# Row statistics of the scan phase on ScalarE instead of VectorE, with one hand-over figure for steps and side work in both phases' orders

## The chip, the cores and the metric

One of the eight cores of a Trainium2 chip runs the whole program. The metric is the device time of one execution in microseconds (us); lower is better. The engines are named as the profile names them: PE is TensorE (PEld its weight loads), DVE is VectorE, ACT is ScalarE, POOL is GpSimd, SP is the engine that issues most DMAs.

## What is computed

Two residual blocks on x of 8 batches x 1024 tokens x 512 channels, all in f32. The first is an attention with 16 heads, whose weights are scaled by the conditioning vector. The second is a gated state-space scan, and the change lies in the computation of `xn` in it:

```python
xr, gate = jnp.split(x @ W_in.T, 2, axis=-1)          # 1024 channels each
xc = silu(conv4(xr + t_emb) + b_conv)
mu = xc.mean(-1, keepdims=True)
var = xc.var(-1, keepdims=True)
xn = (xc - mu) / jnp.sqrt(var + 1e-05) * ln_g + ln_b
Bm, Cm, dt = jnp.split(xn @ W_xproj.T, 3, axis=-1)
dt = jnp.tanh(dt @ W_dt.T + b_dt) * 0.01
Ad = 1.0 + dt * -jnp.tanh(A_log)
Bd = Bm * jnp.minimum(norm(xn), 1.0)
# over the 1024 tokens, state h of 16 x 1024 per batch:
h = clip(h * Ad + Bd * xn_t, -10, 10);  y_t = Cm_t . h
out = (y + D * xn) * silu(gate) @ W_out.T
```

## The kernel before

**Two phases.** `Attention` runs first and `Scan` after it. In each, a planner (`attention_plan`, `scan_plan`) fixes beforehand the order of all pieces of work on every engine. Each engine then works through its own list strictly in order, and waits at a piece until the semaphores of its inputs and buffers have come.

**The scan's steps.** The state of all 8 batches lies on the 128 partitions (8 x 16) with 1024 channels along the row. The recurrence is strictly serial: one step per token, 1024 steps. Step t has four parts.
- `x`, PE line 1794: two matmuls spread the token's row over the partitions, into one of two PSUM buffers (`xps`). It runs two steps ahead, and waits for `q` of step t-2, which frees the buffer.
- `q`, DVE line 2064: state = x * bd + state.
- `g`, DVE line 2070: the clip.
- `out`, PE line 1808: every second step four matmuls contract two states into `yps`; every eighth step ACT evicts that bank (line 1974).

**The side work.** Steps go in 8 chunks of 128 tokens. Beside the steps of chunk i runs side work of two kinds. That of chunk i+1 is its convolution, statistics, projection and rows (`convolve`, `rows`), in two half-batches (`hb`) of four batches (`bb`). That of chunk i-1 is its gates and output projection (`finish`). During the steps all side work has two PSUM banks (`SIDE`). In chunk 0 there is no `finish`, in chunk 7 no `convolve` and no `rows`.

**The statistics of one half-batch.** PE transposes the channels-first result (`t1`, line 1761, 8 groups of four). ACT copies each of the 8 banks to SBUF (`te`, line 1927). DVE takes `bn_stats` of each (`st`, line 2082), `bn_aggr` once per batch (`ag`, line 2087), and adds epsilon (`rs`, line 2096). ACT takes the root (`rsq`, line 1932), DVE the reciprocal and the two factors (`rr`, lines 2100 to 2103). Only then can ACT normalise the rows (`nrm`, line 1938), and DVE finish the projections (`pjo`, lines 2114 and 2117) that PE has left in a bank (`pj`, line 1770).

**What sets the order.** `Order` keeps a modelled clock for each engine and places next the piece that could start first. Each piece has a duration (the second argument of `put`). Side pieces have a due step besides, spread evenly over a range of steps. A piece is ready when its inputs are done, plus a hand-over `lag` if an input comes from another engine; a bank is free a `lag` after its eviction:

```python
engine, end = self.done[piece]
at = max(at, end + (0.0 if engine == item["engine"] else self.lag[item["side"]]))
...
self.free[m] = end + self.lag[item["side"]]
```

`lag` is a pair of microseconds: the first for steps, the second for side work. These figures and the durations are used for the order alone; no instruction carries them.

Of the kernel before, what the change touches and what calls it, by code (L numbers as in the profile page):

```python
# [23 lines left out]
DIN = 1024  # L24
# [5 lines left out]
BANK = 512  # L30
# [1114 lines left out]
def scan_plan(plan, B, NCH, TOK):  # L1145
# [3 lines left out]
    order = Order(plan, 4, (0.2, 0.5))  # L1149
# [46 lines left out]
    def convolve(i, banks, halves=range(2)):  # L1196
        out = []
        put = lambda *a, **k: out.append(item(*a, **k))
        for hb in halves:
# [33 lines left out]
            put("DVE", 0.25, ("rs", i, hb), (("ag", i, hb, HB - 1),) + was("nrm", *old, HB - 1) + was(  # L1233
                "pjo", *old, HB - 1), [("dve_rs", 1)])
            put("ACT", 1.6, ("rsq", i, hb), (("rs", i, hb),), [("act_rs", 1)])
            put("DVE", 0.8, ("rr", i, hb), (("rsq", i, hb),), [("dve_rs", 3)])
# [193 lines left out]
class Scan:  # L1430
    def __init__(self, nc, ctx, d, ident, B, S, first):
# [31 lines left out]
        self.mvb = sb("mvb", [P, HB, 2])  # L1463
        self.rsd = sb("rsd", [P, HB])
# [68 lines left out]
    def dve_signals(self, p):  # L1533
# [4 lines left out]
            "g": "dve_g", "q": "dve_q", "tap": "dve_tap", "st": "dve_st", "ag": "dve_bn", "rs": "dve_rs", "rr": "dve_rs",  # L1538
# [316 lines left out]
    def scalar(self, act):  # L1855
# [5 lines left out]
        for p in plan.pieces:  # L1861
# [59 lines left out]
            elif kind == "te":  # L1921
# [87 lines left out]
    def vector(self, dve):  # L2009
# [6 lines left out]
        for p in plan.pieces:  # L2016
# [72 lines left out]
            elif kind == "rs":  # L2089
                i, hb = at  # L2090
                w.wait_ge(sem["dve_bn"], plan.after("dve_bn", ("ag", i, hb, HB - 1)))
# [4 lines left out]
                dve.tensor_scalar(self.rsd[:, :], self.mvb[:, :, 1], EPS_LN, None, ALU.add).then_inc(sem["dve_rs"], 1)  # L2096
            elif kind == "rr":
# [3 lines left out]
                dve.tensor_scalar(self.nm[:, :], self.mvb[:, :, 0], -1.0, None, ALU.mult).then_inc(sem["dve_rs"], 1)  # L2101
# [228 lines left out]
```

## Time and profile before

| | |
|---|---|
| median of 3 runs | 6392.38 us (6392.36 to 6394.39) |
| the profiled execution | 6391.57 us |
| its span, first to last instruction | 6389.8 us |
| busy: PE / DVE / ACT / POOL | 94 / 71 / 36 / 50 % |
| mean granted PE clock, share of full speed | 0.964 |
| attention with its setup | about 0 to 3345 us |
| the 1024 steps | 3473 to 6299 us |
| the last outputs after the steps | to 6390 us |

Shares of busy time over the whole span mix two phases that have different limits. The page's slices show it: DVE is busy for four to six tenths in the first half and for nine in the second, while PE is at nine in both. So each phase is to be read by itself, and the steps by chunks: their side work repeats from chunk to chunk. [...]

### The profile page before, as it was taken

To read this page: it belongs to the slowest core of one execution; us is meant where nothing else is said; L and a number is where in the kernel's file an instruction comes from. 1 tells how busy PE (TensorE), PEld (TensorE's weight loads), DVE (VectorE), ACT (ScalarE), POOL (GpSimd) and SP (SyncE) were. 2 spreads that over 40 slices of the span, in tenths; PEclk is the share of its full clock that TensorE was granted. 3 is DMA by queue.
4 is the path that set the end of the run, shared out by engine and by line. 5 is a ranking of instruction groups with operands and counts; after the bars stand their busy time and mean duration, and the time that the engine had idled before them with its cause. 6 is when DMAs were issued, how large, how long until landed. Compare 5 with 4: busy or idle time off the path is not lost. (4 is left out here: it accounts for less than half of the span.)

```text
span 6389.8 us, 73140 instructions
## 1 busy us (share of the span) xinstructions
PE 5983.1 (94%) x24000; PEld 2727.2 (43%) x24000; DVE 4526.8 (71%) x5830; ACT 2331.5 (36%) x4460; POOL 3208.2 (50%) x2625
## 2 busy tenths in 40 slices
PE   7999999999999999999986779999999999999998
PEld 3444444444444444444433324444443444444343
DVE  4646556556565555655635999999999999999984
ACT  2444444444444444444444313323232423233111
POOL 1776666767667666675645233424243342424313
PEclk7999999999999999999987989999999999999999
DMA  2332323323233232332214243444444443444433
GB/s 87 84 87 77 95 56 99 87 82 93 60 95 83 82 91 58 96 86 70 72 62 131 65 118 90 141 97 122 117 111 132 100 143 94 126 107 122 116 93 114
DMA packets 411564, 613.29 MB, mean 96 GB/s; under 512 B 58768, under 2 KB 189968, under 8 KB 410672
## 3 DMA queue, kind: packets, MB, share of 16 engines
q1 hardware_dynamic: 374320, 558.24, 31.5%
q10 hardware_dynamic: 36864, 50.38, 3.1%
q8 instruction: 190, 3.11, 0.2%
q14 instruction: 190, 1.56, 0.1%
HBM read 305.31 MB, written 201.38 MB: 79 GB/s over the span
## 5 line engine op out<-in xcount | busy, mean ns | idle before, releaser
L1125 POOL TENSOR_TENSOR acc<-acc,prob 128x512 f32<-128x512 f32 x1536 | 1906.9, 1280 | 920.8 <-PE bank L815 532.3
L1055 DVE TENSOR_REDUCE mx<-bank 128x1 f32<-128x512 f32 x2048 | 1299.2, 683 | 583.8 <-PE bank L785 579.9
L2064 DVE SCALAR_TENSOR_TENSOR g<-xps,bd,g 128x1024 f32<-128x1024 f32 x1024 | 1312.7, 1282 | 156.6 <-PE xps L1794 84.0
L948 ACT ACTIVATE prob<-misc 128x512 f32<-128x512 f32 x1452 | 817.9, 598 | 911.0 <-PE misc L802 732.0
L1794 PE MATMUL xps<-sx,spread 128*128 128x512 f32 x2048 | 888.7, 520 | 181.2 <-DVE g L2064 165.2
L785 PE MATMUL bank<-khat,qhat 96*128 96x512 f32 x2048 | 959.6, 526 | 18.8 <-DVE mx L1055 7.0
L2070 DVE TENSOR_SCALAR g<-g,lim 128x1024 f32<-128x1024 f32 x1024 | 881.0, 860 | 32.3
L802 PE MATMUL misc<-qhat,khat 98*128 98x512 f32 x1642 | 722.5, 475 | 49.2 <-ACT prob L948 43.8
L1794 PEld LDWEIGHTS xps<-sx,spread 128*128 128x128 f32 x2048 | 356.8, 195 | 712.7 <-DVE g L2064 390.5
L1808 PE MATMUL yps<-g,cexp 128*32 128x512 f32 x4096 | 604.8, 640 | 0.0
L785 PEld LDWEIGHTS bank<-khat,qhat 96*128 96x128 f32 x2048 | 384.1, 197 | 497.6 <-issue 383.6
L815 PE MATMUL bank<-prob,V 128*32 128x512 f32 x3584 | 519.5, 628 | 4.3 <-ACT prob L948 4.3
L1751 PE MATMUL miscb<-x2T_sb,w_in 128*128 128x512 f32 x952 | 475.1, 608 | 8.8 <-DMA x2T_sb<-scratch_x2T 8.8
L773 PE MATMUL bank<-xhT,wqk 128*128 128x512 f32 x1024 | 481.6, 602 | 1.0 <-ACT xhT L886 1.0
L802 PEld LDWEIGHTS misc<-qhat,khat 98*128 98x128 f32 x1642 | 312.7, 192 | 363.9 <-ACT prob L948 213.6
L1848 PE MATMUL miscb<-w_out,ygT 128*128 128x512 f32 x928 | 457.0, 603 | 1.4 <-DVE x_t L2168 1.4
L1818 PE MATMUL miscb<-w_in,x2T_t 128*128 128x512 f32 x896 | 434.1, 606 | 1.1 <-DMA x2T_t<-scratch_x2T 1.1
L1074 DVE RECIPROCAL rsum<-rsum 128x512 f32<-128x512 f32 x64 | 214.3, 3349 | 272.3 <-ACT rsum L954 272.3
L2186 POOL TENSOR_TENSOR cexp<-cd,mask 128x256 f32<-128x256 f32 x128 | 79.0, 617 | 648.4 <-DVE g L2070 456.7
L2225 POOL TENSOR_TENSOR y_t<-y_t,dx_t 128x512 f32<-128x512 f32 x118 | 150.7, 1279 | 450.9 <-DVE g L2070 297.0
L1046 DVE SCALAR_TENSOR_TENSOR halves<-bank,qk_dc,halves 128x512 fp32r<-128x512 f32 x128 | 95.7, 748 | 359.3 <-ACT halves L912 359.3
L2193 POOL TENSOR_TENSOR xn<-xn,affine 128x512 f32<-128x512 f32 x128 | 167.2, 1311 | 345.9 <-ACT xn L1938 211.6
(220 smaller groups left out, 6943.1 us busy)
## 6 DMA issues: line engine op xcount, KB each, us to landing
sx<-scratch_xhl SPq DMA_DIRECT2D x512, 128.0 KB, 4.9
scratch_dx<-dx SPq DMA_DIRECT2D x64, 512.0 KB, 2.8
scratch_xhl<-xhi SPq DMA_DIRECT2D x64, 512.0 KB, 4.3
scratch_xhl<-xn SPq DMA_DIRECT2D x64, 512.0 KB, 4.7
scratch_y<-ysb SPq DMA_DIRECT2D x512, 64.0 KB
dx_t<-scratch_dx SPq DMA_DIRECT2D x59, 512.0 KB, 6.1
y_t<-scratch_y SPq DMA_DIRECT2D x59, 512.0 KB, 4.0
xt_n<-in_x SPq DMA_DIRECT2D x112, 256.0 KB, 2.9
```

Source lines behind the costliest of these rows:

```text
L773: mm = pe.matmul(bank[m][:, 0:QC], self.wqk[:, n, it, :], self.xhT[:, it, c * QC:(c + 1) * QC], start=it == 0, stop=it == HT - 1)
L785: pe.matmul(bank[m][:, 0:QC], self.qhat[0:96, s, h, qt * P:(qt + 1) * P], self.khat[0:96, s, h, c * QC:(c + 1) * QC], start=True, stop=Tru ...
L802: pe.matmul(bank[m][:, 0:QC], self.khat[0:98, s, h, kt * P:(kt + 1) * P], self.qhat[0:98, s, h, c * QC:(c + 1) * QC], start=True, stop=Tru ...
L815: mm = pe.matmul(bank[6 + a][h * DH:(h + 1) * DH, 0:QC], self.value(b, kt, g)[:, h * DH:(h + 1) * DH], of, start=kt == 0, stop=kt == TT - 1)
L948: act.activation(to, bank[m][:, 0:QC], ACT.Exp, scale=SCALE).then_inc(sem[f"act_m{m}"], 1)
L1055: dve.tensor_reduce(self.mx2[:, h * TT + qt, c:c + 1], bank[m][:, 0:QC], AX.X, ALU.max).then_inc(sem[f"dve_m{m}"], 1)
L1125: pool.tensor_tensor(self.acc[:, a, h, :], self.acc[:, a, h, :], self.prob[:, (n % 2) * GH + h, :], ALU.add).then_inc(sem["pool_acc"], 1)
L1751: mm = pe.matmul(bank[m][:, :], self.w_in[:, it, ct * P:(ct + 1) * P], self.x2T[:, it, :, :].rearrange("p b q -> p (b q)"), start=it == 0, ...
L1794: mm = pe.matmul(self.xps[t % 2][:, half * BANK:(half + 1) * BANK], self.spread[:, 2 * part + half, :], self.sx[:, n % 2, wd, :], start=Tr ...
L1808: mm = pe.matmul(bank[2 + m][32 * j:32 * (j + 1), :], self.cexp[:, h, tc, :], self.g[:, (t + tp) % 4, half * BANK:(half + 1) * BANK], star ...
L2064: dve.scalar_tensor_tensor(self.g[:, t % 4, :], self.xps[t % 2][:, :], self.bd[:, i % 2, tl:tl + 1], self.g[:, (t - 1) % 4, :], ALU.mult, ...
L2070: dve.tensor_scalar(self.g[:, t % 4, :], self.g[:, t % 4, :], self.lim[:, i % 2, 0, tl:tl + 1], self.lim[:, i % 2, 1, tl:tl + 1], ALU.min, ...
```

## The change

1. In chunks 1 to 7 (`i > 0`) `st` and `ag` are gone from DVE. ACT's copy `te` also gives the sum of each half row (`accum_out`, function Identity in place of Copy). DVE makes the negated mean `nm` of the four batches in two small instructions (`mu`). ACT then squares the centred rows, one ACTIVATE of 128x1024 per batch with the mean as bias and a sum as second output (`sv`); the written squares go to `junk`. `rs` makes the variance from these sums. `rr` has one instruction less, since `nm` exists already. Chunk 0's statistics stay as they were.
2. Both planners take 0.2 us for the hand-over of side work, in place of 0.5.
3. The planner is told of a duration of 0.7 for `te`, 1.06 for each `sv`, 0.25 for `mu`, 0.4 for `rr`.

```diff
-    order = Order(plan, 8, (0.2, 0.5))        # attention_plan
+    order = Order(plan, 8, (0.2, 0.2))
...
-    order = Order(plan, 4, (0.2, 0.5))        # scan_plan
+    order = Order(plan, 4, (0.2, 0.2))
...
-                    put("ACT", 0.6, ("te", i, hb, bb, half), (g,) + was("slo", *old, bb), [("act_m{m}", 1)],
-                        group=g, give=True)
-                    put("DVE", 0.7, ("st", i, hb, bb, half), (("te", i, hb, bb, half),) + (
-                        (("ag", i, hb, bb - 2),) if bb > 1 else ()), [("dve_st", 1)])
-                put("DVE", 0.2, ("ag", i, hb, bb), (("st", i, hb, bb, 1),), [("dve_bn", 1)])
+                    put("ACT", 0.6 if i == 0 else 0.7, ("te", i, hb, bb, half), (g,) + was("slo", *old, bb) + (
+                        was("mu", *old) if i > 1 or i and hb else ()), [("act_m{m}", 1)], group=g, give=True)
...
+                put("DVE", 0.25, ("mu", i, hb), (("te", i, hb, HB - 1, 1),) + was("pjo", *old, HB - 1), [("dve_bn", 2)])
+                for bb in range(HB):
+                    put("ACT", 1.06, ("sv", i, hb, bb), (("mu", i, hb),), [("act_sq", 1)])
+                stats = ("sv", i, hb, HB - 1)
...
+                    act.activation(to, bank[m][:, :], ACT.Identity, accum_out=self.sums[:, bb, half:half + 1]).then_inc(
+                        sem[f"act_m{m}"], 1)
+            elif kind == "sv":
+                i, hb, bb = at
+                w.wait_ge(sem["dve_bn"], plan.after("dve_bn", ("mu", i, hb)))
+                w.wait_ge(sem["act_sq"], plan.before("act_sq", p))
+                w.wait_ge(sem["dve_rs"], plan.after("dve_rs", ("rs", i - 1 + hb, 1 - hb)))
+                act.activation(self.junk[:, :], self.xn[:, bb, :], ACT.Square, bias=self.nm[:, bb:bb + 1],
+                               accum_out=self.dev[:, bb:bb + 1]).then_inc(sem["act_sq"], 1)
...
+                    w.wait_ge(sem["act_sq"], plan.after("act_sq", ("sv", i, hb, HB - 1)))
...
+                    dve.tensor_scalar(self.rsd[:, :], self.dev[:, :], 1.0 / DIN, EPS_LN, ALU.mult, ALU.add).then_inc(
+                        sem["dve_rs"], 1)
+            elif kind == "mu":
...
+                dve.tensor_tensor(self.nm[:, :], self.sums[:, :, 0], self.sums[:, :, 1], ALU.add).then_inc(sem["dve_bn"], 1)
+                w.wait_ge(sem["dve_bn"], plan.after("dve_bn", p) - 1)
+                dve.tensor_scalar(self.nm[:, :], self.nm[:, :], -1.0 / DIN, None, ALU.mult).then_inc(sem["dve_bn"], 1)
```

**What moves in the orders.** First DVE's list during chunk 3, steps 36 and 37 of its 128, where the first half-batch of chunk 4 has its statistics. Before:

```order
L2064 SCALAR_TENSOR_TENSOR g<-xps,bd,g 128x1024
L2082 BN_STATS st<-xn 128x6
L2087 BN_AGGR mvb<-st 128x2
L2070 TENSOR_SCALAR g<-g,lim 128x1024
L2064 SCALAR_TENSOR_TENSOR g<-xps,bd,g 128x1024
L2082 BN_STATS st<-xn 128x6 x2
L2087 BN_AGGR mvb<-st 128x2
L2082 BN_STATS st<-xn 128x6
L2070 TENSOR_SCALAR g<-g,lim 128x1024
L2082 BN_STATS st<-xn 128x6
L2087 BN_AGGR mvb<-st 128x2
L2096 TENSOR_SCALAR rsd<-mvb 128x4
```

And with the change, steps 38 to 42 (the two `nm` rows are `mu`, the `rsd<-dev` row is `rs`, the last row begins `rr`):

```order
L2137 TENSOR_TENSOR nm<-sums 128x4
L2139 TENSOR_SCALAR nm<-nm 128x4
L2096 TENSOR_SCALAR g<-g,lim 128x1024
L2090 SCALAR_TENSOR_TENSOR g<-xps,bd,g 128x1024
L2096 TENSOR_SCALAR g<-g,lim 128x1024
L2090 SCALAR_TENSOR_TENSOR g<-xps,bd,g 128x1024
L2096 TENSOR_SCALAR g<-g,lim 128x1024
L2128 TENSOR_SCALAR rsd<-dev 128x4
L2090 SCALAR_TENSOR_TENSOR g<-xps,bd,g 128x1024
L2096 TENSOR_SCALAR g<-g,lim 128x1024
L2090 SCALAR_TENSOR_TENSOR g<-xps,bd,g 128x1024
L2143 RECIPROCAL rsd<-rsd 128x4
```

The statistics' instructions that stood between the step's are gone. Between `mu` and `rs` now stand three clips and two `q`, and `rs` and `rr` come three steps later than before.

ACT's list at the same half-batch, with the change:

```order
L1945 ACTIVATE xn,sums<-miscb 128x512 x4
L1953 ACTIVATE junk,dev<-xn,nm 128x1024 x4
L2000 ACTIVATE ysb<-yps 128x512
L2030 ACTIVATE ygT<-miscb 128x512
L1958 ACT_TABLE_LOAD
L1958 ACTIVATE rsd<-rsd 128x4
L1964 ACTIVATE xn<-xn,nmr_b,rsd 128x1024 x2
```

The four `sv` stand together, ahead of an eviction of `yps` and one of a side bank. Before, the last copies, one eviction, the table load and the root followed one another. In the whole list of ACT 67 table loads stand with the change, and 53 before.

PE's list with the change, from the `x` of steps 38 and 39 to the `x` of step 44 (`wx,xc` is `pj`, `ident,y_t` a transpose of `finish`; both kinds take a side bank):

```order
L1805 MATMUL xps<-sx,spread 128x512 x4
L1781 MATMUL miscb<-wx,xc 128x48 x4
L1819 MATMUL yps<-g,cexp 32x512 x4
L1805 MATMUL xps<-sx,spread 128x512 x2
L1781 MATMUL miscb<-wx,xc 128x48 x4
L1851 MATMUL miscb<-ident,y_t 128x128 x4
L1805 MATMUL xps<-sx,spread 128x512 x2
L1819 MATMUL yps<-g,cexp 32x512 x4
L1805 MATMUL xps<-sx,spread 128x512 x2
L1781 MATMUL miscb<-wx,xc 128x48 x8
L1805 MATMUL xps<-sx,spread 128x512 x2
L1819 MATMUL yps<-g,cexp 32x512 x4
```

Before, the first two projections stood within one step (8 and 8 matmuls around one `out`), and output matmuls of `finish` followed three steps later; now the second projection waits for a bank some three steps after the first, and PE's list holds little but steps' matmuls in between. Attention's lists move too, by the second part of the change alone, without a piece more or less.

## Rows read from the trace of the kernel before

**Rows 1.** The page, busy time, share and instructions of each engine, whole span
```profile
PE 5983.1 (94%) x24000; PEld 2727.2 (43%) x24000; DVE 4526.8 (71%) x5830; ACT 2331.5 (36%) x4460; POOL 3208.2 (50%) x2625
```

**Rows 2.** Busy time by stretch (start:end, length, engines with counts, PE clock, DMA share, GB/s)
```profile
0.00:3345.00 3345.00, 3195.80 (x12745) 1463.89 (x12746) 1867.77 (x2833) 1435.33 (x2641) 2140.00 (x1729) 0.97 0.28 81
800.00:3200.00 2400.00, 2330.27 (x9486) 1071.20 (x9478) 1378.29 (x2083) 1046.05 (x1919) 1604.36 (x1295) 0.99 0.28 80
3473.00:6299.00 2826.00, 2639.77 (x10758) 1182.19 (x10757) 2597.81 (x2901) 827.69 (x1688) 944.63 (x798) 0.97 0.42 110
```

**Rows 3.** The same view, chunks 0, 3 and 7 of the steps
```profile
3473.00:3810.00 337.00, 257.17 (x1085) 105.80 (x1083) 322.96 (x370) 94.42 (x201) 91.62 (x80) 0.91 0.31 78
4535.00:4896.00 361.00, 345.29 (x1411) 157.16 (x1410) 333.56 (x378) 115.60 (x237) 133.84 (x112) 0.98 0.44 117
5982.00:6297.00 315.00, 308.83 (x1208) 131.79 (x1210) 271.42 (x263) 39.44 (x65) 49.46 (x46) 0.99 0.39 93
```

**Rows 4.** The same view, chunk 3 in eight pieces of 16 steps each
```profile
4535.00:4579.00 44.00, 44.00 (x160) 18.66 (x159) 40.48 (x43) 14.08 (x37) 6.36 (x6) 1.00 0.49 114
4579.00:4623.00 44.00, 43.33 (x166) 18.82 (x165) 41.73 (x45) 13.97 (x38) 6.35 (x6) 1.00 0.28 69
4623.00:4677.00 54.00, 51.95 (x250) 27.32 (x248) 48.68 (x64) 19.44 (x37) 18.20 (x15) 1.00 0.44 102
4677.00:4726.00 49.00, 48.20 (x178) 20.57 (x180) 46.52 (x48) 19.97 (x45) 23.12 (x19) 1.00 0.38 105
4726.00:4773.00 47.00, 45.26 (x205) 23.42 (x202) 45.57 (x64) 20.29 (x41) 19.90 (x18) 0.93 0.54 159
4773.00:4818.00 45.00, 42.12 (x177) 19.18 (x176) 36.70 (x39) 8.89 (x12) 21.59 (x19) 0.92 0.34 83
4818.00:4857.00 39.00, 34.32 (x134) 13.59 (x133) 36.95 (x34) 8.68 (x13) 21.74 (x18) 0.96 0.57 171
4857.00:4896.00 39.00, 36.10 (x153) 15.62 (x152) 36.92 (x47) 10.29 (x16) 16.57 (x14) 1.00 0.48 142
```

**Rows 5.** Waits (engine line <- releaser: us in all, times, longest), chunk 3
```profile
PE xps L1794 <- DVE g L2064: 13.1, 16, 1.9
...
DVE g L2064 <- PE xps L1794: 7.3, 8, 2.8
```

**Rows 6.** Groups by line, VectorE, chunk 3 (busy us, mean ns | idle us before)
```profile
L2082 DVE BATCH_NORM_STATS2 st<-xn 128x6 f32<-128x512 f32 x16 | 10.8, 681 | 0.0
...
L2087 DVE BATCH_NORM_AGGREGATE mvb<-st 128x2 f32<-128x12 f32 x8 | 1.7, 207 | 0.2
...
L2096 DVE TENSOR_SCALAR rsd<-mvb 128x4 f32<-128x4 f32 x2 | 0.3, 170 | 0.1
```

**Rows 7.** VectorE in order of time at the last steps (start us, us)
```profile
6265.52 1.29 DVE L2064 SCALAR_TENSOR_TENSOR g<-xps,bd,g 128x1024 f32<-128x1024 f32 x1
6266.84 0.81 DVE L2070 TENSOR_SCALAR g<-g,lim 128x1024 f32<-128x1024 f32 x1
6267.74 1.28 DVE L2064 SCALAR_TENSOR_TENSOR g<-xps,bd,g 128x1024 f32<-128x1024 f32 x1
```

**Rows 8.** Groups by line, ScalarE, chunk 3
```profile
L1927 ACT ACTIVATE xn<-miscb 128x512 f32<-128x512 f32 x16 | 9.3, 596 | 15.3 <-PE miscb L1761 15.3
...
L1953 ACT ACTIVATE junk<-xn 128x1024 bf16<-128x1024 f32 x8 | 8.4, 1047 | 0.0
...
L1953 ACT ACTIVATION_READ_ACCUMULATOR junk<-xn 128x1 f32 x8 | 1.5, 192 | 0.0
L1932 ACT ACT_TABLE_LOAD x1 | 1.3, 1283 | 0.0
```

**Rows 9.** In order of time: a transpose eviction and the weight load behind it
```profile
4400.48 0.60 ACT L1927 ACTIVATE xn<-miscb 128x512 f32<-128x512 f32 x1 [1.39 <-PE miscb L1761]
...
4401.13 0.42 PEld L1761 LDWEIGHTS miscb<-ident,xc 128*128 128x128 f32 x4 [0.24 <-ACT xn L1927]
```

**Rows 10.** Waits of PE for data, attention from 800 to 3200 us
```profile
PE misc L802 <- ACT prob L948: 29.3, 80, 0.9
```

More of the change, by code:

```diff
@@ L1227, in convolve @@
                     put("PE", 0.45, g, (("silu", i, hb, 4 * half + 3),), [("pe_m{m}", 1)], take=banks, group=g)
[L1228 to L1234 removed]
+                    put("ACT", 0.6 if i == 0 else 0.7, ("te", i, hb, bb, half), (g,) + was("slo", *old, bb) + (
+                        was("mu", *old) if i > 1 or i and hb else ()), [("act_m{m}", 1)], group=g, give=True)
+                    if i == 0:
+                        put("DVE", 0.7, ("st", i, hb, bb, half), (("te", i, hb, bb, half),) + (
+                            (("ag", i, hb, bb - 2),) if bb > 1 else ()), [("dve_st", 1)])
+                if i == 0:
+                    put("DVE", 0.2, ("ag", i, hb, bb), (("st", i, hb, bb, 1),), [("dve_bn", 1)])
+            if i == 0:
+                stats = ("ag", i, hb, HB - 1)
+            else:
+                put("DVE", 0.25, ("mu", i, hb), (("te", i, hb, HB - 1, 1),) + was("pjo", *old, HB - 1), [("dve_bn", 2)])
+                for bb in range(HB):
+                    put("ACT", 1.06, ("sv", i, hb, bb), (("mu", i, hb),), [("act_sq", 1)])
+                stats = ("sv", i, hb, HB - 1)
+            put("DVE", 0.25, ("rs", i, hb), (stats,) + was("nrm", *old, HB - 1) + was("pjo", *old, HB - 1), [("dve_rs", 1)])
             put("ACT", 1.6, ("rsq", i, hb), (("rs", i, hb),), [("act_rs", 1)])
[L1236 removed]
+            put("DVE", 0.8 if i == 0 else 0.4, ("rr", i, hb), (("rsq", i, hb),), [("dve_rs", 3 if i == 0 else 2)])
             for bb in range(HB):
@@ L1254, in rows @@
                 if bb < HB:
-                    put("ACT", 1.06, ("nrm", i, hb, bb), (("rr", i, hb), ("st", i, hb, bb, 1)), [("act_nm", 1)])
+                    put("ACT", 1.06, ("nrm", i, hb, bb), (("rr", i, hb),), [("act_nm", 1)])
                     for half in range(2):
@@ L1463, in __init__ @@
         self.mvb = sb("mvb", [P, HB, 2])
+        self.sums = sb("sums", [P, HB, 2])
+        self.dev = sb("dev", [P, HB])
         self.rsd = sb("rsd", [P, HB])
@@ L1926, in scalar @@
                     w.wait_ge(sem[f"st_xlo{bb}"], plan.after(f"st_xlo{bb}", ("slo", i - 1 + hb, 1 - hb, bb)))
-                act.activation(self.xn[:, bb, half * BANK:(half + 1) * BANK], bank[m][:, :], ACT.Copy).then_inc(
-                    sem[f"act_m{m}"], 1)
+                to = self.xn[:, bb, half * BANK:(half + 1) * BANK]
+                if i == 0:
+                    act.activation(to, bank[m][:, :], ACT.Copy).then_inc(sem[f"act_m{m}"], 1)
+                else:
+                    if i > 1 or hb:
+                        w.wait_ge(sem["dve_bn"], plan.after("dve_bn", ("mu", i - 1 + hb, 1 - hb)))
+                    act.activation(to, bank[m][:, :], ACT.Identity, accum_out=self.sums[:, bb, half:half + 1]).then_inc(
[7 more added lines that the diff above has]
+                               accum_out=self.dev[:, bb:bb + 1]).then_inc(sem["act_sq"], 1)
             elif kind == "rsq":
@@ L2090, in vector @@
                 i, hb = at
-                w.wait_ge(sem["dve_bn"], plan.after("dve_bn", ("ag", i, hb, HB - 1)))
+                if i == 0:
+                    w.wait_ge(sem["dve_bn"], plan.after("dve_bn", ("ag", i, hb, HB - 1)))
+                else:
+                    w.wait_ge(sem["act_sq"], plan.after("act_sq", ("sv", i, hb, HB - 1)))
                 if i or hb:
@@ L2095, in vector @@
                     w.wait_ge(sem["dve_pr"], plan.after("dve_pr", ("pjo", i - 1 + hb, 1 - hb, HB - 1)))
-                dve.tensor_scalar(self.rsd[:, :], self.mvb[:, :, 1], EPS_LN, None, ALU.add).then_inc(sem["dve_rs"], 1)
+                if i == 0:
+                    dve.tensor_scalar(self.rsd[:, :], self.mvb[:, :, 1], EPS_LN, None, ALU.add).then_inc(sem["dve_rs"], 1)
+                else:
+                    dve.tensor_scalar(self.rsd[:, :], self.dev[:, :], 1.0 / DIN, EPS_LN, ALU.mult, ALU.add).then_inc(
+                        sem["dve_rs"], 1)
+            elif kind == "mu":
+                i, hb = at
+                for bb in range(HB):
+                    for half in range(2):
+                        self.of_bank(w, "act", ("t1", i, hb, bb, half), ("te", i, hb, bb, half))
+                w.wait_ge(sem["dve_pr"], plan.after("dve_pr", ("pjo", i - 1 + hb, 1 - hb, HB - 1)))
+                w.wait_ge(sem["dve_rs"], plan.after("dve_rs", ("rr", i - 1 + hb, 1 - hb)))
+                dve.tensor_tensor(self.nm[:, :], self.sums[:, :, 0], self.sums[:, :, 1], ALU.add).then_inc(sem["dve_bn"], 1)
+                w.wait_ge(sem["dve_bn"], plan.after("dve_bn", p) - 1)
+                dve.tensor_scalar(self.nm[:, :], self.nm[:, :], -1.0 / DIN, None, ALU.mult).then_inc(sem["dve_bn"], 1)
             elif kind == "rr":
```

5 lines of the change are left out of this document (3 added, 2 removed).

## The prediction

> **What bounds the kernel now.** The page's busy shares come first [rows 1]: PE 94%, DVE 71%, ACT 36%, POOL 50%. ACT, which gets the work, has the most room. The shares mix two phases, so the busy times by stretch come next [rows 2]. In attention PE is busy 2330.3 of 2400 us and DVE 1378 of them: PE bounds, and what DVE does there is hidden. Over the 2826 us of steps PE has 2639.8 and DVE 2597.8, which says that two engines stand near the limit.
>
> The same view by chunk [rows 3] tells the chunks apart. Chunk 0 has no output work: PE 257 of 337 us, DVE 323. It is DVE's. Chunk 3, which stands for chunks 1 to 6 (361.0 to 363.0 us each), has PE at 345.3 and DVE at 333.6 of 361. Chunk 7 has PE at 308.8 of 315 and no statistics. In eight pieces of 16 steps [rows 4] chunk 3 shows which engine ends last where. In the first four PE leaves 0, 0.7, 2.0 and 0.8 us, and DVE 3.5, 2.3, 5.3 and 2.5. In the fifth both are nearly full. In the last three PE leaves 2.9, 4.7 and 2.9. The waits [rows 5] show the coupling: PE waits 13.1 us for `q` to free a buffer, DVE 7.3 us for `x`; the rest of DVE's 27 us without work are short gaps and waits that this view counts elsewhere. The third and the fifth piece hold the two half-batches' statistics (54 and 47 us where 39 are possible).
>
> **What leaves DVE.** Per half-batch 8 `st` of 0.681 and 4 `ag` of 0.207 go: 5.45 + 0.83 = 6.28 us [rows 6]. `mu` brings two instructions of 128x4 and `rr` loses one; `rs` keeps its size. Net one tiny instruction more, at the 0.170 of the nearest row [rows 6]. That is 6.11 us per half-batch, 12.2 per chunk. Chunks 1 to 7 are prepared beside chunks 0 to 6, so 14 half-batches: **85.5 us less work on DVE**. It lies between the steps' own instructions and nothing else covers it there; the question is what PE lets through.
>
> - *Chunk 0.* PE has 80 us free, so the 12.2 come back almost whole. The longer ACT chain may take a little: 11 us.
> - *Chunks 1 to 6, lower end.* If PE's work stays in its pieces, the two pieces with statistics can shrink only by PE's free time, 2.05 + 1.74 = 3.8 us per chunk [rows 4].
> - *Upper end.* 12.2 per chunk, if PE's side work slips into the last three pieces, where PE has 10.5 us free.
> - *Taken: 7 per chunk, 42 in all*, a little below the middle of 3.8 and 12.2. Side work is due by the step and steps come sooner, so the planner asks PE for the same work in less time. The five early pieces already fill PE, and PE's total of 345.3 us forbids a chunk much under 350 unless switching between kinds of matmul gets cheaper.
> - *Chunk 7.* Only the order changes: 0, with 3 us either way.
>
> **What ACT gets.** Each `te` gains a read of the accumulator, 0.192 [rows 8]; each `sv` is a 128x1024 ACTIVATE with its read, 1.047 + 0.192 = 1.24 us, since `junk<-xn` is the same form. Per half-batch 8 x 0.192 + 4 x 1.24 = 6.5 us, 91 us in all, beside 115.6 us of work in 361 us [rows 3]: hidden. What isn't hidden is latency. DVE's list has `rs` behind `mu` with three clips and two `q` between. At the bare step's pace, 2.22 us [rows 7], those take 0.81 + 2 x 2.22 = 5.25 us. ACT needs 4 x 1.24 = 4.96 and two hand-overs. A hand-over shows as 0.05 us: the eviction ends at 4401.08 and the weight load starts at 4401.13 [rows 9]. So 5.06 against 5.25: the planner counts 1.06 for an `sv` and left out the read, and DVE still just escapes a wait. Behind a waiting `rs` stand all steps, so the bounds are 0 and 1.3 us (one late eviction and its hand-overs) for each of 14; I take 0.2 each, **+3 us**.
>
> ACT's list has 14 table loads more. The row has 1.283 us each [rows 8], 18 us in all in ACT's idle time. Where one stands before the root it delays `rr`, and so the projections' banks, not a step: nothing to 1 us each on PE; it is in the choice of 7. ScalarE: Activation LUTs in the Trainium skill (What ACT_TABLE_LOAD costs) puts a switch at about 2.66 us, since a drain comes with the load; by that the 14 would be 37 us of ACT, still inside its idle time. The trace shows the 1.28 as a row and no drain beside it.
>
> The projections hold both side banks longer, because `rs` and `rr` come three steps later in the list. PE then streams little but `x` and `out` for about three steps, when 2.22 us of step hold some 1 us of step matmuls. That is up to 3 us of PE's time lost per half-batch, and the second reason for 7 instead of 12.
>
> **What the shorter hand-over does.** It changes lists only. The real hand-over of 0.05 us [rows 9] lies below both figures, so 0.2 is nearer the chip, and the old margin of 0.5 kept side work behind its true time. In attention the gain is bounded by PE's free time, 70 of 2400 us, or 97 of 3345 [rows 2]; recovering half would be 48. The loss is bounded by the waits that a too hopeful order makes: PE waits 29.3 us on ACT's evictions in 2400 [rows 10], 41 in 3345, and doubling that costs 41. I take **-10**, small against both, on the side of the truer figure: most of PE's time is matmuls that no order shortens.
>
> **The sum.** -11 - 42 + 3 - 10 = -60 us. The profiled execution took 6391.6 us (span 6389.8), so 6331.6; the median of the three runs is 0.8 above it. **Predicted: 6332 us.** Under 0.2%, about 13 us, a measurement of this kernel can't be told from no change.
>
> **Rivals.**
> 1. *PE keeps it.* Side work doesn't slip; chunks 1 to 6 give 3.8 each, chunk 0 gives 11, attention nothing: 34 us, 6358. For it: PE is at 345 of 361. Against it: PE has 10.5 us free in each chunk's last pieces.
> 2. *DVE is the true bound, and all of its saving returns.* 85 us from the steps, 10 from attention and up to 25 more where the truer hand-overs close waits: about 6285. For it: the spacing of matmuls is tighter than their busy time, so that part of PE's 345 us is overlap. Against it: DVE waits in the pieces where PE is fullest. Trainium Kernel Development and Optimization in the Trainium skill (Best Practices) says to judge TensorE by weight-load busy share and not by the matmul busy share; the weight loads here are at 43% [rows 1], which would leave PE far from its limit and is this rival's case.
> 3. *The statistics' chain eats it.* If ACT is later than modelled by more than the 0.2 us of slack, `rs` holds all steps. It gives back the saving whole at 6.1 us per half-batch, that is if about five more evictions came ahead of the four `sv`. The list has them in a block. Then 6385 to 6392, with attention 0. The same time would stand for a change that, in effect, only renames who waits.
> 4. *Slower: attention's order.* PE serves its list in order, and a score matmul waits for a bank that ACT must free; its waits are now 80 in 2400 us and 0.37 us long on average [rows 10]. If 0.2 us is too hopeful for side evictions queued behind exponentials, and such waits grow threefold, that is +82 us; less rival 1's 34 it ends at 6440. It decides against the change from about 0.5 us more on each of these waits. Against it: the steps have had 0.2 all along, and those waits are short.
>
> **How the numbers follow.** Forecast 0.52, with its own range from 6305 to 6355; rival 1 0.20; rival 2 0.17; rival 3 0.05; rival 4 0.06. The range of 8 in 10 takes in rivals 1 and 2 and leaves out the last two with the outer edge of rival 2: 6280 to 6376. Faster by over 0.2%: the first three less a little at rival 1's edge, 0.88. Within 0.2%: 0.06. Slower: 0.06.
>
> **What would show it.** The steps' stretch about 50 us shorter: chunk 0 near 326 us, chunks 1 to 6 near 355, chunk 7 near 315. `bn_stats` absent from DVE in them. PE's free time in chunk 3 down from 16 us to about 10, with DVE's busy time near 322. The wait of `rs` for ACT's `junk` under 0.5 us each. ACT busy about 16 us more per chunk with its table loads. Attention's end within 30 us of 3345, earlier rather than later. I am wrong in the main term if chunks 1 to 6 fall below 350 or stay above 359, and wrong about hand-overs if attention moves by more than 30 us.

## The result, and the profile after

The changed kernel takes 6301.2 us at the median of 4 runs (6295.5 to 6310.6), the kernel before 6393.4 (6392.4 to 6410.6, 4 runs). The ratio is 0.985, with a 95% interval from 0.983 to 0.987: faster by 1.5%, or 92 us, where 60 were forecast. The profiled execution took 6298.7 us, its span 6296.9.

The page's shares hardly moved (busy time, share of the span and instructions of each engine, changed kernel):

```profile
PE 5920.8 (94%) x24000; PEld 2714.3 (43%) x24000; DVE 4471.5 (71%) x5676; ACT 2409.9 (38%) x4698; POOL 3216.4 (51%) x2625
```

ACT has 78 us more than before, DVE 55 less, PE 62 less with the same 24000 matmuls [rows 1]. By stretch, in the view of [rows 2] (attention's middle, then the steps):

```profile
800.00:3200.00 2400.00, 2322.57 (x9545) 1070.24 (x9544) 1380.60 (x2071) 1045.95 (x1941) 1620.00 (x1308) 0.98 0.29 82
3432.00:6206.00 2774.00, 2611.22 (x10758) 1173.89 (x10757) 2532.61 (x2746) 920.86 (x1926) 953.66 (x798) 0.98 0.43 112
```

The steps run from 3432 to 6205 us and last 2772.5 us from the first `q` to the last; before they lasted 2824.5. By chunk, the view of [rows 3], chunks 0, 3 and 7:

```profile
3432.00:3762.00 330.00, 260.46 (x1094) 108.38 (x1092) 313.41 (x349) 108.10 (x235) 91.68 (x80) 0.89 0.32 80
4473.00:4828.00 355.00, 341.89 (x1410) 156.76 (x1409) 324.86 (x358) 128.92 (x271) 135.58 (x112) 0.98 0.45 118
5892.00:6205.00 313.00, 306.62 (x1210) 130.89 (x1210) 270.36 (x263) 39.29 (x65) 49.44 (x46) 1.00 0.38 94
```

And chunk 3 in eight pieces of 16 steps, the view of [rows 4]:

```profile
4473.00:4517.00 44.00, 44.00 (x161) 18.74 (x160) 40.63 (x44) 14.02 (x37) 6.34 (x6) 1.00 0.50 115
4517.00:4563.00 46.00, 45.82 (x175) 19.48 (x177) 44.12 (x49) 14.06 (x39) 6.36 (x6) 1.00 0.35 75
4563.00:4616.00 53.00, 51.40 (x242) 28.04 (x235) 41.57 (x49) 24.47 (x47) 18.34 (x15) 0.94 0.41 97
4616.00:4664.00 48.00, 47.22 (x171) 19.77 (x170) 45.96 (x47) 21.18 (x54) 23.10 (x18) 1.00 0.38 107
4664.00:4707.00 43.00, 42.12 (x195) 20.69 (x196) 40.75 (x48) 22.34 (x49) 21.17 (x18) 1.00 0.53 164
4707.00:4750.00 43.00, 40.42 (x192) 20.11 (x191) 37.83 (x45) 14.11 (x19) 19.75 (x16) 1.00 0.40 95
4750.00:4789.00 39.00, 34.68 (x135) 14.16 (x133) 36.95 (x34) 8.68 (x13) 23.96 (x20) 0.91 0.58 171
4789.00:4828.00 39.00, 36.21 (x151) 15.77 (x150) 37.04 (x48) 10.06 (x16) 16.54 (x14) 0.96 0.46 140
```

The third piece had DVE at 48.7 of 54 us and has it now at 41.6 of 53: DVE lost 7 us of work there and the piece 1 us. The fifth went from 47 to 43, the sixth from 45 to 43. The early pieces are as full on PE as before.

Stages, each from the same marks in every trace: attention's last reciprocal (DVE line 1074 of the kernel before), first and last `q`, last instruction.

| us | before | changed | difference | forecast |
|---|---|---|---|---|
| attention's last reciprocal at | 3278.8 | 3245.2 | -33.6 | -10 |
| from there to the first `q` | 194.0 | 187.0 | -7.0 | 0 |
| chunk 0 | 337.7 | 329.4 | -8.3 | -11 |
| chunks 1 to 6 together | 2171.7 | 2130.2 | -41.5 | -42 |
| chunk 7 | 315.0 | 313.0 | -2.0 | 0 |
| after the last `q` | 92.6 | 92.2 | -0.4 | 0 |

(The forecast's further +3 us was for DVE waiting at `rs`. Each stage is read from one profiled execution; two kernels with the same order of the scan differ by 0.3 and 3.2 us in the steps, below.) So the steps came in total as forecast, and what the forecast lacked lies ahead of them.

### The profile page after: what moved, and what is told of

The parts are those of the page before. It is cut to its first block and busy times, and to the rows that moved or that the text cites. A ratio compares the mean times of both kernels' runs of the same rounds, so it can differ in the third digit from the quotient of the medians.

```text
span 6296.9 us, 73255 instructions
## 1 busy us (share of the span) xinstructions
PE 5920.8 (94%) x24000; PEld 2714.3 (43%) x24000; DVE 4471.5 (71%) x5676; ACT 2409.9 (38%) x4698; POOL 3216.4 (51%) x2625
## 5 line engine op out<-in xcount | busy, mean ns | idle before, releaser
L1805 PE MATMUL xps<-sx,spread 128*128 128x512 f32 x2048 | 908.9, 528 | 143.8 <-DVE g L2090 129.0
L948 ACT ACTIVATE prob<-misc 128x512 f32<-128x512 f32 x1293 | 725.0, 599 | 820.6 <-PE misc L802 695.3
L802 PE MATMUL misc<-qhat,khat 98*128 98x512 f32 x1467 | 626.0, 472 | 28.8 <-ACT prob L948 23.3
L1819 PE MATMUL yps<-g,cexp 128*32 128x512 f32 x4096 | 583.5, 627 | 0.1
L802 PEld LDWEIGHTS misc<-qhat,khat 98*128 98x128 f32 x1467 | 278.5, 192 | 267.5 <-ACT prob L948 115.3
L1909 ACT ACTIVATE xr<-miscb,temb 128x128 f32<-128x128 f32 x476 | 135.6, 368 | 556.1 <-PE miscb L1762 556.1
```

The costliest lines, as they stand in the source:

```text
L802: pe.matmul(bank[m][:, 0:QC], self.khat[0:98, s, h, kt * P:(kt + 1) * P], self.qhat[0:98, s, h, c * QC:(c + 1) * QC], start=True, stop=Tru ...
L948: act.activation(to, bank[m][:, 0:QC], ACT.Exp, scale=SCALE).then_inc(sem[f"act_m{m}"], 1)
L1805: mm = pe.matmul(self.xps[t % 2][:, half * BANK:(half + 1) * BANK], self.spread[:, 2 * part + half, :], self.sx[:, n % 2, wd, :], start=Tr ...
L1819: mm = pe.matmul(bank[2 + m][32 * j:32 * (j + 1), :], self.cexp[:, h, tc, :], self.g[:, (t + tp) % 4, half * BANK:(half + 1) * BANK], star ...
```

## The experiments

Twelve kernels ran. The theory to test was A: the statistics' move shortens the steps, and the shorter hand-over shortens attention because it is nearer to the chip's. The rivals are told with each.

**1 to 3: the three parts apart.** The first changes one figure, the second another, the third is the change with both figures put back:

```diff
# 1, in the kernel before
-    order = Order(plan, 8, (0.2, 0.5))
+    order = Order(plan, 8, (0.2, 0.2))
# 2, in the kernel before
-    order = Order(plan, 4, (0.2, 0.5))
+    order = Order(plan, 4, (0.2, 0.2))
# 3, in the changed kernel
-    order = Order(plan, 8, (0.2, 0.2))
+    order = Order(plan, 8, (0.2, 0.5))
-    order = Order(plan, 4, (0.2, 0.2))
+    order = Order(plan, 4, (0.2, 0.5))
```

> The kernel before with one figure changed: 0.2 us for side work's hand-overs in attention's order alone. Theory A (the shorter figure pays in attention by itself, through its order): the last normalisation of attention starts 30 to 36 us earlier than before, the steps keep their 2824 us, the whole is at 6353 to 6363 us. Rival (attention's gain in the changed kernel came with the scan's order or from run to run scatter): attention within 10 us of before, the whole within 10 us of 6393.

Measured: ratio 0.9935 (0.992 to 0.995). Attention's last reciprocal starts at 3238.8, 40 us earlier than before and so 4 more than the theory allowed; the steps last 2824.8 us. The rival falls.

> The kernel before with one figure changed: 0.2 us for side work's hand-overs in the scan's order alone; statistics stay on VectorE. Theory A (in the steps the statistics' move does the work, the figure moves pieces only): steps 2815 to 2830 us against 2824 before; up to 8 us less between attention's end and the first step; whole 6380 to 6395. Rival (the shorter figure makes a good part of the steps' 52 us): steps at or below 2805 us.

Measured: ratio 0.9967 (0.9954 to 0.998). Steps 2811.0 us, from attention's end to the first `q` 189.5. That is 13.5 us off the steps with the statistics still on DVE: more than the theory gave, less than the rival's.

> The changed kernel with both figures back at 0.5 us: the statistics' move alone. Theory A: steps 2770 to 2785 us (40 to 55 less than before), attention as before, whole 6340 to 6355. Rival (the move needs the shorter figure, since the two banks are held by the later chain): steps at 2800 us or more, whole above 6365.

Measured: ratio 0.9947 (0.9931 to 0.9964). Steps 2793.0 us, chunks 1 to 6 at 357.0 each, attention as before; the median of 6361.4 is worse than the theory's 6355.

The three ratios multiply to 0.985, the whole change's: the parts add. In the steps the move alone gives 31.5 us and the figure alone 13.5, 45 of the 52; the rest needs both. Most visible is chunk 0, which gives 0.5 us with the figure alone, 0.7 with the move alone, and 8.3 with both. In chunks 1 to 6 the parts don't add: the move alone gives 29.5 us, the figure alone 16.4, both together 41.6.

**4: the planner told the truth.** In the changed kernel:

```diff
-                    put("ACT", 1.06, ("sv", i, hb, bb), (("mu", i, hb),), [("act_sq", 1)])
+                    put("ACT", 1.24, ("sv", i, hb, bb), (("mu", i, hb),), [("act_sq", 1)])
-                    put("ACT", 0.6 if i == 0 else 0.7, ("te", i, hb, bb, half), (g,) + was("slo", *old, bb) + (
+                    put("ACT", 0.6 if i == 0 else 0.79, ("te", i, hb, bb, half), (g,) + was("slo", *old, bb) + (
```

> The changed kernel whose planner counts the statistics on ScalarE as the trace shows them: 1.24 us for each squaring with its read in place of 1.06, 0.79 for each copy in place of 0.7. Theory that VectorE waits for the squarings in the changed kernel because the planner has them too short (the third of eight pieces of 16 steps has VectorE idle for 9.9 us): that idle time falls by 2 us or more in each of six chunks, whole 10 to 25 us under the changed kernel's. Rival (the idle time is PE's doing, who does the projections late and serves x behind them): steps within 6 us of the changed kernel's 2772.

Measured: steps 2779.0 us, no gain; ratio 0.9856 (0.9841 to 0.987), the same as the changed kernel's. The planner puts `rs` later, so that in chunks 1 to 6 it now stands 1.4 to 1.7 us behind ACT's last read. The third piece leaves DVE idle for 8.5 to 9.4 us in four of these chunks and for 15 in the other two, 11.1 on the mean, and for 10.4 in the changed kernel. The squarings weren't what DVE waited for. The changed kernel in order of time shows it, in chunk 3 (start us, us, then the idle time before):

```profile
4578.05 0.17 DVE L2139 TENSOR_SCALAR nm<-nm 128x4 f32<-128x4 f32 x1
...
4578.26 1.15 ACT L1953 ACTIVATE junk<-xn,nm 128x1024 bf16<-128x1024 f32 x1 [1.87 <-DVE nm L2139]
...
4583.14 0.18 ACT L1953 ACTIVATION_READ_ACCUMULATOR junk<-xn,nm 128x1 f32 x1
...
4583.36 0.17 DVE L2128 TENSOR_SCALAR rsd<-dev 128x4 f32<-128x4 f32 x1
...
4583.71 0.59 ACT L2030 ACTIVATE ygT<-miscb 128x512 f32<-128x512 f32 x1
...
4584.35 2.65 PE L1781 MATMUL miscb<-wx,xc 128*128 128x48 f32 x16 [1.01 <-ACT ygT L2030]
...
4593.69 1.88 PE L1781 MATMUL miscb<-wx,xc 128*128 128x48 f32 x16
...
4595.61 0.26 DVE L2158 SCALAR_TENSOR_TENSOR proj<-gw,nm,miscb 128x48 f32<-128x48 f32 x1 [5.06 <-PE miscb L1781]
...
4597.20 1.88 PE L1781 MATMUL miscb<-wx,xc 128*128 128x48 f32 x16
...
4599.12 0.26 DVE L2158 SCALAR_TENSOR_TENSOR proj<-gw,nm,miscb 128x48 f32<-128x48 f32 x1 [2.61 <-PE miscb L1781]
...
4599.60 0.81 DVE L2096 TENSOR_SCALAR g<-g,lim 128x1024 f32<-128x1024 f32 x1
```

ACT's four squarings with their reads take from 4578.26 to 4583.32, 5.06 us. DVE, kept busy by three clips and two `q`, comes to `rsd` at 4583.36, 5.14 us after the end of `mu`, and goes on at once. The forecast had 5.06 for ACT's chain and 5.25 for DVE's; here both end within 0.05 us of each other. What is late is the projections. The second needs the bank that `ygT` empties, and that eviction stood behind the squarings (PE idle for 1.01 us at 4584.35). The third comes at 4593.69, the fourth at 4597.20, and DVE waits 5.06 and 2.61 us for them, between the `q` and the clip of one step. Part of the longer wait is PE's clock, which this list doesn't show: the granted clock is 1.00 from 4580 to 4584 us, with PE busy for 2.92 of the 4, then 0.68, and 0.50 from 4588 to 4592. That is the lower of its two levels, 1.2 in place of 2.4 GHz. The four chunks with such a stretch there (1, 2, 3 and 5) have a longest wait of 5.1 us and 10.1 in all, the two without it 2.9 and 2.5, with 7.1 and 6.2 in all. In chunks 1 to 6 these waits are now the largest of DVE's, changed kernel:

```profile
DVE proj L2158 <- PE miscb L1781: 53.8, 18, 5.1
DVE g L2090 <- PE xps L1805: 29.9, 38, 2.1
```

Kernel before:

```profile
DVE g L2064 <- PE xps L1794: 46.1, 54, 2.8
DVE proj L2114 <- PE miscb L1770: 24.3, 16, 2.5
```

DVE's waits for projections grew by 29.5 us over six chunks, its waits for `x` fell by 16.

**5: without the squarings.** The changed kernel leaves the variance out and uses chunk 0's again:

```diff
-                for bb in range(HB):
-                    put("ACT", 1.06, ("sv", i, hb, bb), (("mu", i, hb),), [("act_sq", 1)])
-                stats = ("sv", i, hb, HB - 1)
+                stats = ("mu", i, hb)
...
-                    dve.tensor_scalar(self.rsd[:, :], self.dev[:, :], 1.0 / DIN, EPS_LN, ALU.mult, ALU.add)
+                    dve.tensor_scalar(self.rsd[:, :], self.mvb[:, :, 1], 1.0, EPS_LN, ALU.mult, ALU.add)
```

> The changed kernel without the squaring pass: the variance is left out and chunk 0's is used again, so that ScalarE has 5 us less per half-batch ahead of the root. Theory B (the later chain costs: banks held by the projections, and VectorE's waits for them): steps 10 to 25 us under the changed kernel's 2772, most of it in chunks 1 to 6, VectorE's waits for the projections in them down from 54 us to under 30. Rival (the chain is hidden; VectorE would wait for PE anyway): steps within 6 us.

Measured: ratio 0.987 (0.985 to 0.9889, 2 runs); steps 2788.1 us, 16 us *longer* than with the squarings, though ACT has 5 us less in each chain. Both expectations fell. DVE's waits, the same view of chunks 1 to 6:

```profile
DVE g L2088 <- PE xps L1803: 41.6, 28, 2.8
DVE proj L2156 <- PE miscb L1779: 34.4, 30, 1.6
```

The waits for projections did fall, by 19 us, and those for `x` grew by 12, those for the output matmuls by 14. With pieces taken out, the planner wrote another order; what the order did outweighs what the pieces cost. This kernel can't price the chain.

**6 and 7: other figures in both orders of the changed kernel**, 0.35 and 0.05 in place of 0.2.

> The changed kernel with 0.35 us in both orders. Theory A (the nearer the figure to the chip's hand-over the better): attention's last normalisation between 3245 and 3280, near 3262; steps between 2772 and 2793. Rival (each figure just draws another order, good or bad by luck): attention or steps outside these, below 3238 or above 3285, below 2765 or above 2800.

Measured: attention's last reciprocal at 3226.2, earlier than at 0.2; steps 2823.5 us, all of the move's gain gone. Ratio 0.9909 (0.9889 to 0.9928).

> The changed kernel with 0.05 us for side work in both orders, the hand-over that the trace shows. Theory A as it stands (nearer is better): attention at or below 3240 and steps at or below 2772. Rival (at 0.05 the order leaves nothing for the pipeline's delay of a matmul and runs into short waits): attention above 3255. Rival of luck: any value, without a slope over 0.05, 0.2, 0.35, 0.5.

Measured: attention at 3294.2, later than at 0.5; steps 2810.2. Ratio 0.9988 (0.9977 to 0.9998). Here DVE does wait for the copies that end just ahead of `mu`, which no other run's list shows among the larger waits (same view):

```profile
DVE nm L2137 <- ACT xn L1945: 15.2, 12, 2.3
```

**8: projections counted longer.** In the changed kernel:

```diff
-                    put("PE", 0.9, ("pj", i, hb, bb, q), (("silu", i, hb, CT - 1), ("sgo", 0), ("sgo", 1)) + scaled, [("pe_m{m}", 1)] if q else [],
+                    put("PE", 1.4 if i else 0.9, ("pj", i, hb, bb, q), (("silu", i, hb, CT - 1), ("sgo", 0), ("sgo", 1)) + scaled, [("pe_m{m}", 1)] if q else [],
```

> The changed kernel whose planner counts 1.4 us instead of 0.9 for each half of a projection on PE, so that VectorE's finishing of it stands later and PE is asked for less around it. Theory C (PE is late at the projections, and VectorE stands waiting for them between two instructions of a step): waits of VectorE for projections in chunks 1 to 6 fall from 54 us to under 35, steps 8 to 20 us shorter than 2772, whole 6280 to 6292. Rival (PE's total decides, the wait moves to x): steps within 6 us of 2772, with the waits for x grown by as much.

Measured: steps 2782.9 us, 10 more; ratio 0.9894 (0.9877 to 0.991). The profiled execution was the fastest of four, 6302.4 us with a granted clock of 0.969, while their median is 6321.6: the other three took 14 to 32 us more, with granted clocks of 0.962 to 0.965. DVE's waits in chunks 1 to 6:

```profile
DVE g L2090 <- PE xps L1805: 46.9, 50, 2.1
DVE proj L2158 <- PE miscb L1781: 36.7, 18, 6.0
DVE x_t L2212 <- PE miscb L1859: 14.9, 12, 2.3
DVE cv L2103 <- ACT cv L1919: 7.3, 7, 1.2
```

The waits for projections fell from 53.8 to 36.7 and came back under other names: for `x`, for the output matmuls, for ACT. Theory C falls; the rival is right about where the waits go, though not in its 6 us. Removing a wait by way of the planner's figures moves everything else too.

**9 and 10: the kernel before at other figures**, to compare both homes of the statistics at equal figures, with two more of attention's on the way.

```diff
# 9, in the kernel before
-    order = Order(plan, 8, (0.2, 0.5))
+    order = Order(plan, 8, (0.2, 0.3))
-    order = Order(plan, 4, (0.2, 0.5))
+    order = Order(plan, 4, (0.2, 0.35))
# 10, in the kernel before
-    order = Order(plan, 8, (0.2, 0.5))
+    order = Order(plan, 8, (0.2, 0.4))
-    order = Order(plan, 4, (0.2, 0.5))
+    order = Order(plan, 4, (0.2, 0.05))
```

> The kernel before, statistics on VectorE, with 0.35 us in the scan's order and 0.3 in attention's. If the figure of 0.35 makes a bad order of the scan whoever takes the statistics: steps above 2840 us, that is 20 to 40 over the 2823.5 that the changed statistics had at 0.35. If each order is a draw of its own: steps anywhere from 2805 to 2840, and perhaps no longer than 2823.5. Attention at 0.3: between 3226 and 3240 if time runs smoothly with the figure from 0.2 to 0.35.

> The kernel before, statistics on VectorE, with 0.05 us in the scan's order and 0.4 in attention's. Theory (the statistics' move is worth 30 to 40 us of steps on the mean over orders): steps 2835 to 2855 against 2810 with the changed statistics at 0.05. Rival (draws hide it): steps under 2825. Attention at 0.4: between 3226 and 3280, near 3244, if time runs smoothly with the figure.

Measured: ratios 0.9951 (0.9935 to 0.9966) and 0.9953 (0.9937 to 0.9969), 3 runs each. With the runs above, in us:

| figure for side work | 0.5 | 0.4 | 0.35 | 0.3 | 0.2 | 0.05 |
|---|---|---|---|---|---|---|
| attention's last reciprocal at | 3277 to 3282 | 3244 | 3226 | 3268 | 3235 to 3245 | 3294 |
| steps, statistics on DVE | 2824.5 | | 2806.8 | | 2811.0 | 2838.8 |
| steps, statistics on ACT | 2793.0 | | 2823.5 | | 2772.5 | 2810.2 |
| difference | -31.5 | | +16.7 | | -38.5 | -28.6 |

An order repeats well: four kernels with attention's old order lie within 5 us, five with the new one within 11, two at 0.35 within 1. In the steps the kernel before and experiment 1 have the same order (2824.5 and 2824.8 us), and so have the changed kernel and experiment 11 (2772.5 and 2775.7). But between orders there is no slope. Attention at 0.3 is 23 to 42 us later than at its neighbours 0.35 and 0.2. Theory A's reason, that nearer to the chip's hand-over is better, falls: each figure draws another order, and the draws lie up to 69 us apart in attention and up to 51 in the steps with the statistics on ACT. Over the four figures the statistics' move is worth 20 us on the mean, and once it costs 17. Experiment 10's theory of 30 to 40 on the mean falls with that, though its own steps came within its range.

**11: the best draw of each phase.** Attention's figure at 0.35, the rest as changed:

```diff
-    order = Order(plan, 8, (0.2, 0.2))
+    order = Order(plan, 8, (0.2, 0.35))
```

> The changed kernel with 0.35 us in attention's order and 0.2 kept in the scan's: the best of each as measured. The two orders do not touch: attention's last normalisation at 3224 to 3230, steps at 2770 to 2782, whole 6278 to 6292, 8 to 20 us under the changed kernel.

Measured: 6286.8 us at the median (6282.8 to 6294.6), ratio 0.983 (0.9816 to 0.9845). Attention at 3225.5, steps 2775.7 us, both as they were alone. It computes the same result and is the fastest of all: some 14 us under the changed kernel by the medians, with intervals that overlap.

**12: DVE's saving alone, nothing moved.** In the kernel before every instruction stays where it is, but the statistics of chunks 1 to 7 read 8 elements of each half row, so they are those of 16 of the 1024 channels:

```diff
-                dve.bn_stats(self.st6[:, bb % 2, half, :], self.xn[:, bb, half * BANK:(half + 1) * BANK])
+                dve.bn_stats(self.st6[:, bb % 2, half, :], self.xn[:, bb, half * BANK:half * BANK + (8 if i else BANK)])
```

> The kernel before with every instruction in the same place, but each bn_stats of chunks 1 to 7 reads 8 elements in place of 512 (the statistics are then those of 8 channels). It takes some 65 of 85 us from VectorE and gives ScalarE nothing. Theory D (in a fixed order PE lets through only what it has free where the statistics stand): chunks 1 to 6 at 357 to 359.5 us against 362.0, chunk 0 at 327 to 330 against 337.7, steps 2790 to 2805. Rival (in a fixed order all of it arrives): chunks 1 to 6 at 353 or less, steps 2755 to 2765. Second rival (a new order is needed for any gain): steps above 2812.

Measured: ratio 0.9908 (0.9891 to 0.9926). Groups by line, VectorE, chunk 3:

```profile
L2082 DVE BATCH_NORM_STATS2 st<-xn 128x6 f32<-128x8 f32 x16 | 2.5, 162 | 0.5 <-ACT xn L1927 0.5
```

So 16 x (0.681 - 0.162) = 8.3 us leave DVE per chunk, 58 in the seven. The steps last 2772.9 us, 51.6 less: chunks 1 to 6 are at 354.3, 7.7 less each, chunk 0 gives 3.9. Theory D said 357 to 359.5 for them and falls, and so does the second rival. The first rival named 353 or less and is off by 1.3, but it is the nearest: in a fixed order nine tenths of the saving arrive in the time. The expectation's 65 us of saving were themselves 58. The third and fifth pieces and the whole of chunk 3 (the view of [rows 4]):

```profile
4604.00:4656.00 52.00, 51.26 (x251) 27.29 (x249) 44.72 (x65) 19.80 (x38) 18.45 (x15) 1.00 0.46 109
4705.00:4748.00 43.00, 42.30 (x212) 21.32 (x206) 41.20 (x62) 19.69 (x40) 19.78 (x17) 1.00 0.55 165
4515.00:4869.00 354.00, 340.93 (x1415) 155.31 (x1414) 325.76 (x379) 115.56 (x237) 134.29 (x112) 0.99 0.45 120
```

The third piece had 2.05 us free on PE before and shrank by 2: what PE had free is what it let through. The fifth had 1.74 free and shrank by 4, and PE's busy time in it fell by 3. The granted clock tells why. It was 0.93 over that piece before and is 1.00 here. In the kernel before, in order of time (the views of [rows 2] and [rows 7], PE):

```profile
4755.19 1.06 PE L1808 MATMUL yps<-g,cexp 128*32 128x512 f32 x8
...
4758.00:4762.00 4.00, 3.35 (x20) 1.50 (x18) 3.96 (x7) 1.22 (x3) 1.85 (x2) 1.00 0.43 162
4762.00:4766.00 4.00, 3.13 (x23) 2.65 (x24) 3.96 (x8) 1.17 (x2) 1.42 (x2) 1.00 0.23 76
4766.00:4770.00 4.00, 4.00 (x20) 2.16 (x19) 3.79 (x7) 0.20 (x1) 1.41 (x3) 0.57 0.64 139
4770.00:4774.00 4.00, 4.00 (x16) 2.93 (x20) 3.80 (x8) 2.38 (x2) 1.15 (x2) 0.50 1.00 172
...
4768.00 1.94 PE L1808 MATMUL yps<-g,cexp 128*32 128x512 f32 x8
```

PE had been busy for 6.5 of 8 us; then the clock fell to its lower level for 10.2 us, and the same eight `out` matmuls took 1.94 us in place of 1.06. In chunks 2 to 6 of the kernel before the clock falls at this same place, and in experiment 12 it never does. In all, by the clock's records in the traces, chunks 1 to 6 have 106 us at the lower level before (a granted clock of 0.976) and 51 in experiment 12 (0.988). The other executions agree: their clocks over the whole program are 0.960 to 0.965 before and 0.966 to 0.970 here, on the same chip.

So PE's busy time for the same matmuls in the same order fell by 31 us in the six chunks (2071.5 to 2040.1), and most of that is the clock. One `out` matmul is recorded with 0.593 us at full clock and 1.061 at the lower level (medians), so each us at the lower level costs some 0.44; 55 of them fewer are about 24 us, an estimate. Another 15 us are idle time of PE that closed, and some 7 are left. The clock's share is not an extra to DVE's saving: nothing else was changed, so shortening DVE's work is what moved the times, and with them the clock. But how much would have arrived with the clock held the same, no run separates.

## Why the prediction was right, and where its steps were not

- **What leaves DVE:** 6.11 us per half-batch. `bn_stats` and `bn_aggr` are gone from chunks 1 to 7, and DVE's busy time in chunk 3 fell from 333.6 to 324.9: 8.7 of the 12.2 us. The durations of its instructions, added up, fell by 11.9; the difference is overlap, since the records of neighbouring instructions overlap by 10.0 us in the chunk before and by 7.4 after.
- **7 per chunk in chunks 1 to 6:** measured 6.9. That it fits so well is partly luck. The forecast gave all of it to the statistics; the move alone gave 4.9 (362.0 to 357.0), and the rest came with the hand-over figure, to which the forecast gave nothing in the steps. At 0.35 the same move lost time. The lower bound's reason, that a piece shrinks by what PE has free, held in experiment 12's third piece. What was left out is the clock: "PE's total of 345.3 us" contains about 17 us at the lower level, and the total shrinks when they become fewer. (Chunk 3 of the changed kernel has 17 as well and 3.4 us less busy time on PE, in another order; why isn't known.) In chunks 1 to 6 the changed kernel has 65 us at the lower level where the kernel before has 106. What held the gain below 12.2 isn't shown. DVE waits for projections, 54 us in six chunks for 24 before; the prediction named this as PE's loss, and it shows as DVE's. But experiments 5 and 8 shortened these waits and gained nothing.
- **The clock and the draws.** The same 0.44 us per us at the lower level fits two of the draws with the statistics on DVE: at 0.2 and at 0.35 chunks 1 to 6 gained 16 and 20 us, and they have 41 and 55 us fewer at the lower level, worth 18 and 24. It doesn't fit the third: at 0.05 they lost 11, with 3 more. That is an estimate by size; no run changed the clock alone.
- **Rival 2's case:** 6301 us lies nearer its 6285 than the forecast's 6332, and 4 us outside the forecast's own range from 6305. It isn't rival 2 that came, though: it had 85 us from the steps, and they gave 52. That matmuls start closer together than their recorded time is so: eight of `w_out` at 4744.60 us in the kernel before take 3.60 us, at 0.600 each. The page of the Trainium skill named there (Trainium Kernel Development and Optimization, Best Practices) says to judge TensorE's distance to its limit by MFU, the matmul work done as a share of what is possible, and by weight-load busy share, not by matmul busy share. The trace agrees as far as that overlap goes. The other half of the case, that PE is far from its limit, these traces don't bear out: with DVE's work cut in a fixed order, DVE still waits for PE about as long as before (for `x` 43.3 us in chunks 1 to 6, before 46.1).
- **Chunk 0:** 8.3 for 11. The reason given, PE's 80 us free, was not sufficient: with the move alone it gave 0.7. There DVE waited 5.3 us for projections, with PE's granted clock at its lower level for 16 us of the piece (0.84 over 49 us, where the same piece has 0.94 before and in the changed kernel); whether the clock made the waits or they the clock wasn't tried.
- **ACT:** the squaring with a bias takes 1.150 us, not the 1.047 of its neighbour without one. Changed kernel, chunk 3, groups by line:

```profile
L1953 ACT ACTIVATE junk<-xn,nm 128x1024 bf16<-128x1024 f32 x8 | 9.2, 1150 | 3.4 <-DVE nm L2139 3.2
...
L1945 ACT ACTIVATION_READ_ACCUMULATOR xn<-miscb 128x1 f32 x16 | 3.1, 196 | 0.0
...
L1953 ACT ACTIVATION_READ_ACCUMULATOR junk<-xn,nm 128x1 f32 x8 | 1.5, 186 | 0.0
```

  Its 1.15 + 0.19 make 1.28 from start to start, since they overlap a little, and the chain of four 5.06 us, without its two hand-overs. DVE does not wait at `rs`; the +3 us were not paid. ACT's busy time in chunk 3 rose by 13.4 us, for 16 named. A table load is 1.283 us as before, and the traces have 84 of them in the whole program for 70, 14 more as counted.
- **The hand-over, -10:** this is the term that was mis-sized, and the one that made 60 out of 92. Attention gave 33.6 us in the profiled run and 34 to 44 in the five kernels that share the order; the stretch between the phases gave 7 that the sum didn't have. By the prediction's own sign, a move of attention by more than 30 us, it was wrong about hand-overs. The bounds of -48 and +41 held, but PE's free time in 3345 us is 149 by [rows 2], not the 97 that the 70 of 2400 were scaled up to. The argument, a truer figure closes waits, did not: at 0.3 attention gains only 11 us, and at 0.05 it loses 15. Nor did PE's waits by name fall. In attention from 800 to 3200 us, changed kernel:

```profile
PE bank L792 <- DVE mx L1063: 30.7, 22, 3.5
PE misc L802 <- ACT prob L948: 17.6, 34, 2.9
```

  The wait on evictions fell from 29.3 [rows 10] to 17.6, the one of the maxima's transpose (PE line 792) rose from 12.7, in the same view of the kernel before, to 30.7. The gain is in PE's busy time again, 2974.7 to 2944.5 us between attention's first and last reciprocal, while the idle time stayed at about 102. It isn't the clock: PE spent 120 us of that stretch at the lower level before and 133 after. What in the new order shortens it stays open.
- **Rivals 3 and 4** did not come about. An order of attention slower than the old one exists, as rival 4 held possible: at 0.05, by 15 us.

## What to carry to other kernels

Where a planner fixes the order, any edit of its pieces or figures is two edits: the cost of the pieces, and a new draw of the order. Here draws spread over 50 to 70 us in a phase, as much as the work removed; so price the work in a fixed order first (experiment 12), and then try a handful of figures for each phase by itself, since the phases add (experiment 11). PE's busy time is no floor: read the granted clock of the stretch beside it, in both kernels, before putting a difference down to work or to waiting.

## What the runs showed of the hardware

- A 128x1024 f32 squaring on ACT with a per-row bias and an accumulated sum took 1.150 us against 1.047 without the bias; the read of the accumulator took 0.186 to 0.196 each time.
- `bn_stats` of 128x8 took 0.162 us and of 128x512 0.681.
- Eight 128x512 matmuls of `out` took 1.06 us where the granted clock was 1.00 and 1.94 where it was 0.50. In five chunks of the kernel before the clock fell at the same place; in chunk 3 that was after 8 us in which PE was busy for 6.5.
- When only DVE's instructions were shortened, PE's time at the lower clock in chunks 1 to 6 went from 106 to 51 us and its busy time for the same instructions in the same order from 2071.5 to 2040.1.
